# First layer of a graph network: sums with 128 features as one stationary operand, two steps behind the candidates, and a one-hot with lanes innermost

## What is computed

```python
zmax = jnp.max(z, axis=-1, keepdims=True)
e0 = e[:, 0, :]
e1 = e[:, 1, :]
q = GAMMA * zmax[src] * e1 + e0
sum_q = jax.ops.segment_sum(q, dst, num_segments=n)
sum_ac = jax.ops.segment_sum(e1, dst, num_segments=n)
z_new = BETA * z + (1.0 - BETA) * sum_q / (sum_ac + 1e-06)
...
x = _layernorm(x + _L0_gnn_ref(x, edge_attr3_2x64, src, dst), axis=-1)
x = _layernorm(x + _L1_gnn_ref(x, L1_gnn_Wq, L1_gnn_Wk, L1_gnn_Wv, L1_gnn_Wout, edge_index), axis=-1)
```

## Time and profile before

| | |
|---|---|
| median of 3 runs | 2995.58 us (2989.38 to 2998.26) |
| profiled execution, its own time | 2992.95 us |
| its span | 2991.2 us |
| mean granted clock of TensorE | 0.704 |
| busy over the span: PE, DVE, ACT, POOL | 2188.7, 1762.0, 1316.8, 1863.8 us |
| first layer's loop | 112 to 738 us |

### The profile page before, as it was taken

One profiled execution on the slowest core, in us unless ns is written; L12 is line 12 of the kernel. 1 busy time (PEld: TensorE's weight loads), 2 busy tenths in 40 slices (PEclk: granted clock), 3 DMA queues, 4 the chain that ended last, 5 costly groups with the idle time before them and its releaser, 6 DMA issues.

```text
span 2991.2 us, 78102 instructions
## 1 busy us (share of the span) xinstructions
PE 2188.7 (73%) x25208; PEld 1580.3 (53%) x25209; DVE 1762.0 (59%) x5859; ACT 1316.8 (44%) x3754; POOL 1863.8 (62%) x2579
## 2 busy tenths in 40 slices
PE   0476676667738686787788877878779877879875
PEld 0455565556713454555565554655546555556655
DVE  2676766666262565555555565555555565656568
ACT  0443433343116444544444454444445454545443
POOL 1355555554114767777777777777777777777750
PEclk9988887787556867667656677566675666766577
DMA  1455555553110222212222121222221222212111
GB/s 43 148 182 166 182 164 165 166 170 116 22 27 16 42 40 42 43 36 42 43 43 42 36 47 38 43 43 43 43 43 35 43 42 42 43 35 47 38 21 23
DMA packets 175515, 197.69 MB, mean 66 GB/s; under 512 B 94963, under 2 KB 97699, under 8 KB 173025
## 3 DMA queue, kind: packets, MB, share of 16 engines
q1 hardware_dynamic: 124838, 138.90, 16.3%
q0 software_dynamic: 50048, 51.35, 9.3%
HBM read 184.87 MB, written 5.25 MB: 64 GB/s over the span
## 4 chain that ended last, share of the span: by engine, by line
POOL 33%; PE 27%; issue 20%; DVE 9%; DMA 5%; SPq 2%; ACT 2%; DVEq 1%; ACTq 0%; POOLq 0%
POOL XS L456 32%; DMA XS<-x_dram,dst_bs 5%; PE psN L1135 3%; PE psS L1281 3%; PE psM L1240 3%; PE psV L1240 3%; PE psM L1135 2%; PE psX L1126 2%; PE psV L1126 2%; PE psT L1235 1%; POOL XS L405 1%; DVE O L728 1%; DVE zm L623 1%; PE psN L1230 1%; PE psX L1230 1%
## 5 line engine op out<-in xcount | busy, mean ns | idle before, releaser
L456 POOL DMA_INDIRECT XS<-x_dram,dst_bs x1564 | 1494.9, 956 | 585.6 <-issue 444.9
L725 DVE SCALAR_TENSOR_TENSOR l_st<-l_st,alpha,rsum 64x1 f32 x782 | 170.3, 218 | 534.3 <-PE psV L1240 281.3
L1281 PE MATMUL psS<-XT,Ubuf 96*128 96x512 f32 x522 | 418.0, 896 | 19.8 <-ACT Ubuf L987 19.3
L797 DVE TENSOR_REDUCE rmax<-psS 128x1 f32<-128x512 f32 x391 | 270.4, 692 | 114.1 <-PE psS L1281 81.5
L1240 PEld LDWEIGHTS psV<-XS,PT 128*128 128x128 f32 x1568 | 287.3, 273 | 1.5 <-ACT PT L1036 1.2
L1240 PE MATMUL psV<-XS,PT 128*128 128x64 f32 x1568 | 286.9, 348 | 0.7 <-ACT PT L1036 0.7
L1240 PEld LDWEIGHTS psM<-XS,dst_bs 128*128 128x128 f32 x1560 | 284.6, 272 | 1.6 <-ACT dst_bs L1036 1.6
L1240 PE MATMUL psM<-XS,dst_bs 128*128 128x64 f32 x1560 | 283.7, 346 | 0.7 <-ACT dst_bs L1036 0.7
L1036 ACT COPY dst_bs<-psT 128x512 f32<-128x512 f32 x195 | 114.3, 586 | 345.8 <-PE psT L1235 344.2
L1036 ACT COPY PT<-psT 128x512 f32<-128x512 f32 x196 | 114.9, 586 | 340.1 <-PE psT L1235 339.5
L1230 PEld LDWEIGHTS psX<-ident,XS 128*128 128x128 f32 x392 | 59.1, 185 | 385.8 <-issue 385.2
(11 more groups left out here) (267 smaller groups left out, 4386.2 us busy)
## 6 DMA issues: line engine op xcount, KB each, us to landing
big<-in_edge_attr_2x SPq DMA_DIRECT2D x195, 512.0 KB, 4.0
big<-dst_turned SPq DMA_DIRECT2D x49, 512.0 KB
XS<-x_dram,dst_bs POOLq DMA_INDIRECT x1564, 2.4
O<-codes_dram SPq DMA_DIRECT2D x200, 6.0 KB
x_dram<-x SPq DMA_DIRECT2D x1, 1568.0 KB, 8.8
out<-big SPq DMA_DIRECT2D x12, 128.0 KB
codes_dram<-O SPq DMA_DIRECT2D x3, 392.0 KB
dst_turned<-big SPq DMA_DIRECT2D x1, 784.0 KB
```

The source lines that it names most:

```text
L456: pool.indirect_dma_start(xs(k, j), None, x1_dram, bass.IndirectOffsetOnAxis(ap=idx2[b % SB][:, k * CPP + j:k * CPP + j + 1], axis=0)).the ...
L725: dve.scalar_tensor_tensor(out=ls, in0=ls, scalar=al[half], in1=rs[half], op0=ALU.mult, op1=ALU.add)
L797: dve.tensor_reduce(rmax[:, q:q + 1], psSc[q][:, :], AX_X, ALU.max)
L1281: pe.matmul(psSc[1 - a][:, :], Ubuf[1 - a][:, :], XT[(J - 1) % 3][:, :], start=True, stop=True).then_inc(s_done, 1)
```

## The change

- The stationary operand of the sums is all 128 features at once, so that 8 matmuls a step take the place of 32; all of them stream the whole 48 columns of `hz`.
- PE computes sums(t-2) in step t, not sums(t-1). DVE adds the sums of step t-3, not t-2. `hz` gets four buffers (`HB4`) in place of two, and the counts of the semaphores, the wait of SP for its slot and the end of the loop are moved to match. SP still loads the edges of step t after the sums of step t-7. DVE's L593 now waits for sums(t-3).
- `lane_ids` and `hi_hot` are stored with the 49 lanes innermost. The product L617 then reads both operands side by side, and the comparison L597 has its second operand, one value for each of the 8 columns, repeated over the innermost 49.

```diff
...
     SB = 3
+    HB4 = 4
     U2 = 48
...
     TP_ = NC // CPP
...
         hi_i = XS[0:TP_, 0:RE].bitcast(I32)
-        hz = [XS[:, k * SJ * 2 * W:(k + 1) * SJ * 2 * W].rearrange("p (j w) -> p j w", j=SJ) for k in range(3)]
-        hzX = hz[2]
+        hz = [XS[:, k * SJ * 2 * W:(k + 1) * SJ * 2 * W].rearrange("p (j w) -> p j w", j=SJ) for k in range(HB4)]
         dst_bs = sb("dst_bs", [P, 4 * CH], I32)
...
                 if not (isinstance(t, int) and t < S1):
-                    sp.wait_ge(seg_done, seg0 + (t - S1 + 3))
+                    sp.wait_ge(seg_done, seg0 + (t - S1 + 4))
                 load_edges(t, k % S1)
...
             pool.wait_ge(s_const, 2)
-            pool.iota(lane_ids, [[1, LANES], [0, SJ]], base=0, channel_multiplier=0,
+            pool.iota(lane_ids, [[0, SJ], [1, LANES]], base=0, channel_multiplier=0,
                       allow_small_or_imprecise_dtypes=True)
...
                 h1 = part[:, 4 * W:6 * W].rearrange("p (h w) -> p h w", h=2)
-                hot4 = hz[k % 2].rearrange("p (h j) w -> p h j w", h=2)
+                hot4 = hz[k % HB4].rearrange("p (h j) w -> p h j w", h=2)
                 vv = pool.snap(pcc, min_val=1)
...
                 pool.wait_ge(zm_done, vv)
-                weighed(hz[k % 2], zm[k % 4]).then_inc(hz_done, 1)
+                weighed(hz[k % HB4], zm[k % 4]).then_inc(hz_done, 1)
                 pool.tensor_tensor(h2, hot4[:, :, 0:2, 0:W], hot4[:, :, 2:4, 0:W], ALU.add).then_inc(deg_read, 1)
...
-            for s, n in ((sel_done, 2), (hz_done, 1), (half_added, 2), (add_done, 3), (seg_done, 2), (deg_read, 2), (deg_done, 1), (s_pass, 1)):
+            for s, n in ((sel_done, 2), (hz_done, 2), (half_added, 3), (add_done, 4), (seg_done, 3), (deg_read, 2), (deg_done, 1), (s_pass, 1)):
                 dve.sem_inc(s, n)
...
             def hi_hots(t, q):
-                dve.tensor_tensor(hi_hot[q].rearrange("p (w j) -> p w j", j=SJ), lane_ids.rearrange("p (w j) -> p w j", j=SJ),
-                                  hi_col[:, bass.ds(t, 1), :].broadcast_to([P, LANES, SJ]), ALU.is_equal).then_inc(hi_done, 1)
+                dve.tensor_tensor(hi_hot[q].rearrange("p (j w) -> p j w", j=SJ), lane_ids.rearrange("p (j w) -> p j w", j=SJ),
+                                  hi_col[:, bass.ds(t, 1), :].rearrange("p s j -> p (s j)").unsqueeze(2).broadcast_to([P, SJ, LANES]), ALU.is_equal).then_inc(hi_done, 1)
...
-                sums_of = not (isinstance(t, int) and t < 2)
+                sums_of = not (isinstance(t, int) and t < 3)
                 vv = dve.snap(tc, min_val=1)
-                if sums_of and k % 2 == 0:
-                    dve.load(lo_d, visits[0:1, bass.ds(t * 2 - 4, 4)])
+                if sums_of and k % 2 == 1:
+                    dve.load(lo_d, visits[0:1, bass.ds(t * 2 - 6, 4)])
                 if sums_of:
-                    la, lb = lows(k)
+                    la, lb = lows(k + 1)
                 dve.wait_ge(z_done, vv)
                 dve.wait_ge(hi_done, vv)
-                dve.tensor_tensor(picked[k % 2].rearrange("p (j w) -> p j w", j=SJ), psZ[k % 2][:, 0:SJ * LANES].rearrange("p (j w) -> p j w", j=SJ),
-                                  hi_hot[k % 2].rearrange("p (w j) -> p j w", j=SJ), ALU.mult).then_inc(sel_done, 1)
+                dve.tensor_tensor(picked[k % 2], psZ[k % 2][:, 0:SJ * LANES], hi_hot[k % 2], ALU.mult).then_inc(sel_done, 1)
                 dve.wait_ge(seg_done, vv)
                 dve.wait_ge(deg_read, vv)
-                hots(hz[k % 2][:, :, 0:W], rel_of(t)).then_inc(hot_done, 1)
+                hots(hz[k % HB4][:, :, 0:W], rel_of(t)).then_inc(hot_done, 1)
                 dve.wait_ge(hot_done, vv)
...
                 if sums_of:
-                    add_sums(la, psG[k % 2], 0).then_inc(half_added, 1)
+                    add_sums(la, psG[(k + 1) % 2], 0).then_inc(half_added, 1)
                 hi_hots(t + 1, (k + 1) % 2)
...
                     dve.wait_ge(half_added, vv)
-                    add_sums(lb, psG[k % 2], 1).then_inc(add_done, 1)
+                    add_sums(lb, psG[(k + 1) % 2], 1).then_inc(add_done, 1)
                 dve.reg_add(tc, tc, 1)
...
                             sums_step(i * UN + (HEAD + k), HEAD + k)
+                v0 = dve.snap(tc, min_val=1)
+                last_sums(NS - 3, v0)
                 dve.load(lo_d, visits[0:1, NC - 4:NC])
-                v0 = dve.snap(tc, min_val=1)
-                v1, v2 = dve.snap(v0 + 1, min_val=1), dve.snap(v0 + 2, min_val=1)
+                v1 = dve.snap(v0 + 1, min_val=1)
+                v2, v3 = dve.snap(v1 + 1, min_val=1), dve.snap(v1 + 2, min_val=1)
                 now = dve.snap(over, min_val=1)
-                last_sums(0, v0)
-                last_sums(1, v1)
-                dve.wait_ge(add_done, v2)
+                last_sums(NS - 2, v1)
+                last_sums(NS - 1, v2)
+                dve.wait_ge(add_done, v3)
                 dve.sem_inc(s_passd, 1)
...
                     h, c = j // CPP, j % CPP
-                    for q in range(4):
-                        n = W if q < 2 else 2 * W
-                        last = pe.matmul(ps[q * QT:(q + 1) * QT, h * 2 * W:h * 2 * W + n], e_sb[slot][:, h, c, q * QT:(q + 1) * QT],
-                                         buf[:, j, 0:n], start=(c == 0), stop=(c == CPP - 1))
+                    last = pe.matmul(ps[:, h * 2 * W:(h + 1) * 2 * W], e_sb[slot][:, h, c, :], buf[:, j, :], start=(c == 0), stop=(c == CPP - 1))
                 last.then_inc(done, 1)
...
                 pe.wait_ge(ld1[k % S1], loaded)
-                sums_of(k % S1, hz[k % 2], psG[k % 2], seg_done)
+                sums_of(k % S1, hz[k % HB4], psG[k % 2], seg_done)
                 if k % S1 == S1 - 1:
...
                 lanes(k)
-                if not (isinstance(t, int) and t < 1):
-                    sums_step(k - 1, vv)
+                if not (isinstance(t, int) and t < 2):
+                    sums_step(k - 2, vv)
                 if k % 2 == 0:
...
                             step(i * UN + (HEAD + k), HEAD + k)
-                sums_step(NS - 1, pe.snap(pc, min_val=1))
+                left = pe.snap(pc, min_val=1)
+                sums_step(NS - 2, left)
+                sums_step(NS - 1, pe.snap(left + 1, min_val=1))
...
             pe.wait_ge(s_all1, 2)
```

## The result

| | before | after |
|---|---|---|
| median | 2995.08 us | 3307.94 us (3307.46 to 3311.13, 4 runs) |
| ratio | | 1.105, 95% interval 1.103 to 1.107 |
| span of the profiled execution | 2991.2 us | 3309.3 us |
| first layer's loop | 626 us | 945 us |
| what follows the loop | 2253 us | 2252 us |

The account below looks back on a forecast made before the run. PE, torn by reading its own program, bounds the first layer's loop. At half clock 196 x 4.7 = 921 us plus 25 for returns make 946 against 626: 2993 + 320 = 3313 us, range 3280 to 3370.

Parts of the forecast that it names:

- The bound before: First layer's loop, 3.19 us a step: PE pauses inside matmul groups, awaiting its own program, once in 125 load-matmul pairs.
- missing tears: PE's pauses for its program in the loop, coming every third step after the change; costed at nothing beyond five returns.
- A pair goes by its load: Sums on PE: the weight load sets a pair's time; 16 pairs take 1.75 us at full clock, 3.30 at half.
- the third rival: Loads not slowed at half clock: 0.105 us a pair in the loop, 2992 us, no change; chance 0.03.
- The level of the clock: First layer's loop begins at half clock and stays there, PE's step being 4.7 us.
- The step and the returns: Loop: 196 steps of 4.7 us, plus 4.9 us idle at each of five returns to the 28-step body's top, 946 us.
- DVE and POOL: Loop: DVE goes from 2.21 to 2.11 us a step, POOL stays at 1.71, both covered by PE.
- Two steps behind: Loop: PE's 1.06 us wait for POOL's product ahead of the sums goes to zero, already within the terms.
- The first, full clock: New sums raise the clock in the loop: PE's step 2.63 us, total 2929 us (2906 to 2960); chance 0.13.
- The second, full clock until the first return: Loop at full clock for 56 steps, then half clock for 140: +204, 3197 us; chance 0.11.
- The fourth, tears that remain at full clock: Program fetch, not PE, sets the loop's pace: 90 us on top of a full-clock loop, 3019 us; chance 0.03.

Follow-up runs that it names:

- doubled stream: Changed kernel with each of the sums' matmuls streaming its 48 columns twice, the second copy unread: 2931.1 us, one execution.
- warm start: Changed kernel with five dense f32 matmuls of 512 columns, output unread, ahead of the first layer's loop: 3201.1 us, one execution.

## Why the prediction was right, point by point

- **The bound before.** PE, torn by the reading of its own program, was said to set the pace. Right, and the experiments show it better than the trace did: removing POOL's waits (the change without its wide sums) and DVE's time (the new layout alone) changed nothing, removing instructions did. One thing had been underrated. The forecast counted on no gain from the missing tears because PE would be full; with two groups of 64, an edit on PE alone, the kernel gained 94 us, by fewer tears and by the higher clock that came with them.
- **A pair goes by its load.** 0.200 to 0.215 us at half clock were taken from the second layer and the fold. Measured 3.43 to 3.56 us for 16, 0.214 to 0.222, against 3.30 taken. The rows were right at their upper end. The 0.200 of the second layer was read from start to start of two groups, and the next group there begins 0.10 us after the last of the eight loads. Inside the group the loads are as far apart as here: eight of them span 1.83 us and the last takes 0.333, so seven distances of 0.214. A group of 16 has fewer such joints for its length. The doubled stream confirms that the stream lies beneath the load at half clock (3.50 us for 16 pairs). "TensorE: Matmul & The Clock Gate" in the Trainium skill, section LDWEIGHTS, gives columns / 1.2 ns without a level: it fits at full clock and is half of what this loop shows at half clock, so the third rival is out.
- **The level of the clock.** Expected at half from the first step and staying there. Right, by the spans.
- **The step and the returns.** 4.70 us a step and 25 us of returns made 946; it was 945. Two terms were mis-sized and cancel. The step is 4.79: sums 0.13 to 0.26 more, lanes 1.00 and not 1.11, as the first load of the sums starts 0.18 us before the lanes' end; in all 196 x 0.09 = +17 us. The returns cost little over 1 us each and not 4.9, as PE waits there for 5.7 us in all:

```profile
PE psV L1127 <- issue: 5.7, 5, 1.5
```

  The kernel before has 4.94 us for one, and the doubled stream at full clock 14.7 us for five. That a slower PE has more of its program in store when it comes to the return fits these three numbers, but no run tests it.
- **DVE and POOL.** DVE was put at 2.11 us a step and has 411 / 196 = 2.10, and the two operations at 0.56 each were 0.567 and 0.559. POOL was said to be unchanged at 1.71; it has 369 / 196 = 1.88, from L405. PE covered it at 4.8 us.
- **Two steps behind.** Counted at nothing, under a full PE. Right for this kernel (the wide sums alone lose as much), and for a reason that the prediction did not give, also with the narrow sums: the tears take back what the wait returns.
- **The rivals.** The first, full clock, was put at 2929 us and needed something to raise the clock: with the stream doubled 2931 us were measured, and PE's step there is 2.67 against 2.63. That the two totals are so close is in part luck: the returns took 14.7 us there, not 25. The 10 us of half clock that the rival put behind each return were 10 to 14. The second, full clock until the first return, was put at 3197: 3201 with the warm start. Neither happens by itself. (Where slower begins, the prediction says some 50 steps at half clock; its own working gives 42.) The fourth, tears that remain at full clock, is out for 42 pairs a step: 0.4 us of them with the doubled stream.

## What to carry to other kernels

Cut PE's instructions where its groups are torn at equal counts, but look at what the load of the stationary operand costs then: here two halves side by side won 4% where one whole lost 10%. A full PE at half clock can be a state that it does not leave; try whether more streamed columns under the same loads, which cost nothing beneath them, bring the clock back. And read the level of the clock from spans of known instructions, not from the column alone.

## What the runs showed of the hardware that was not expected

- The clock has a memory in this loop. The same instructions ran 140 us at full clock after a dense start, and 670 us at half clock after one idle time of 3.16 us; 96 instead of 48 columns streamed moved it up without help.
- Loads of 64 f32 columns that go to the two halves of the array by turns and loads of 128 differ by nearly two for the same 128 features: 32 pairs in 1.88 us against 16 in 3.43, both at half clock.
- A comparison of bf16 values on DVE goes from 355 to 559 ns when its second operand is repeated over the innermost dimension and not the outermost, and a POOL operation of 0.23 us that starts beside it lasts until it ends, 0.53.
- DVE's product fell from 873 to 567 ns by reading its one-hot side by side instead of in steps of 16 bytes.
